# Tail of a GAT, GCN and LSTM kernel: which pairs are summed in PSUM, and where additions and stores stand

## The reference

```
h = jnp.maximum(_layernorm(x), 0.0)
x = x + _L0_gnn_ref(h, adj, W, a)             # graph attention
h = jnp.maximum(_layernorm(x), 0.0)
x = x + _L1_gnn_ref(h, adj, ...)
# _L1_gnn_ref: two graph convolutions give h, then
for p in range(1, 5):                         # windows of p nodes
    last = _lstm_last(Wih[p-1], Whh[p-1], bih[p-1], bhh[p-1], windows(h, p))
    h = h.at[:, idx, :].set(last)             # the last node of each window
```

## Time and profile before

| | |
|---|---|
| median of 3 runs | 450.65 us (450.28 to 450.68) |
| the profiled execution, own time | 451.49 us |
| its span | 449.5 us |
| outside the span | 1.99 us |
| PE busy | 426.2 us (95%) |
| DVE busy | 376.1 us (84%) |
| ACT busy | 333.6 us (74%) |
| last round, its first product on PE | 395.03 us |
| last gate product on PE | 436.63 us |

### The profile page before, as it was taken

One profiled execution on the slowest core, in us unless ns is written; L12 is line 12 of the kernel. 1 busy time (PEld: TensorE's weight loads), 2 busy tenths in 40 slices (PEclk: granted clock), 3 DMA queues, 4 the chain that ended last, 5 costly groups with the idle time before them and its releaser, 6 DMA issues.

```text
span 449.5 us, 7890 instructions
## 1 busy us (share of the span) xinstructions
PE 426.2 (95%) x2472; PEld 369.0 (82%) x2472; DVE 376.1 (84%) x994; ACT 333.6 (74%) x651; POOL 67.3 (15%) x145
## 2 busy tenths in 40 slices
PE   5689999979999999999999999999999999999995
PEld 4468788878888888888778888899999988887884
DVE  5999999987778787877778888878888789888995
ACT  3779999966899999897787768667767675574552
POOL 3678442240411313100000000000000000000000
PEclk9989999989999999999999999999999999999999
DMA  8910000000000000000000000000000000002116
GB/s 244 335 56 1 1 3 0 0 1 0 2 0 2 0 0 0 0 0 0 1 1 1 0 1 1 0 2 0 1 1 1 2 0 0 1 23 71 47 47 188
DMA packets 14212, 11.67 MB, mean 26 GB/s; under 512 B 1123, under 2 KB 12390, under 8 KB 13926
## 3 DMA queue, kind: packets, MB, share of 16 engines
q1 hardware_dynamic: 12118, 10.11, 7.5%
q10 hardware_dynamic: 2064, 1.18, 1.0%
HBM read 7.10 MB, written 4.19 MB: 25 GB/s over the span
## 4 chain that ended last, share of the span: by engine, by line
PE 69%; DVE 21%; ACT 4%; issue 3%; DMA 1%; DVEq 1%; POOL 0%; ACTq 0%; POOLq 0%
PE ps L1044 45%; PE ps L1188 12%; PE ps L1192 6%; DVE score L760 5%; DVE score L726 4%; DVE xs L774 3%; DVE stats L675 2%; PE ps L1090 2%; DVE stats L716 2%; ACT v_norm L510 1%; PE ps L1024 1%; ACT work L635 1%; PE ps L1135 1%; DMA xs<-in_x 1%; PE ps L1114 1%
## 5 line engine op out<-in xcount | busy, mean ns | idle before, releaser
L635 ACT ACTIVATE work<-ps,bl 128x512 f32<-128x512 f32 (+2 forms) x204 | 111.1, 628 | 26.9 <-PE ps L1192 19.3
L1044 PE MATMUL ps<-h_hi,wl_hi 128*128 128x512 f32 (+3 forms) x252 | 93.5, 371 | 0.9 <-DVE xs L916 0.8
L1044 PE MATMUL ps<-h_hi,wl_lo 128*128 128x512 f32 (+3 forms) x252 | 92.8, 368 | 0.0
L1044 PE MATMUL ps<-h_lo,wl_hi 128*128 128x512 f32 (+3 forms) x252 | 92.7, 368 | 0.0
L625 ACT ACTIVATE work<-work 128x512 f32<-128x512 f32 (+2 forms) x56 | 31.5, 571 | 45.1 <-DVE work L911 34.6
L510 ACT ACTIVATE v_norm<-xs,shift,scale 128x128 f32 (+1 forms) x128 | 52.7, 490 | 2.6 <-POOL shift L425 2.6
L1044 PEld LDWEIGHTS ps<-h_hi,wl_hi 128*128 128x128 f32 x252 | 47.5, 188 | 8.3 <-issue 1.2
L1044 PEld LDWEIGHTS ps<-h_lo,wl_hi 128*128 128x128 f32 x252 | 47.4, 188 | 6.6
L1044 PEld LDWEIGHTS ps<-h_hi,wl_lo 128*128 128x128 f32 x252 | 47.5, 188 | 5.6
L1188 PE MATMUL ps<-s_hi,wl_hi 128*128 128x512 f32 (+2 forms) x144 | 51.7, 362 | 0.0
L1188 PE MATMUL ps<-s_hi,wl_lo 128*128 128x512 f32 (+2 forms) x144 | 51.2, 358 | 0.0
(11 more groups left out here) (136 smaller groups left out, 911.7 us busy)
## 6 DMA issues: line engine op xcount, KB each, us to landing
result<-xs SPq DMA_DIRECT2D x12, 256.0 KB, 2.3
work<-in_w_ih_t SPq DMA_DIRECT2D x1, 1024.0 KB, 10.4
work<-in_w_hh_t SPq DMA_DIRECT2D x1, 1024.0 KB, 9.4
xs<-in_x SPq DMA_DIRECT2D x2, 256.0 KB, 3.8
xs<-in_x SPq DMA_DIRECT2D x1, 512.0 KB, 7.2
result<-xs SPq DMA_DIRECT2D x4, 128.0 KB, 2.5
result<-xs ACTq DMA_DIRECT2D x4, 128.0 KB, 2.8
adj_raw<-in_adj ACTq DMA_DIRECT2D x1, 256.0 KB, 6.8
```

Source lines behind the costliest of these rows:

```text
L635: nc.scalar.activation(lw[:, par, g, 0:cols], ps[:, 4 * par + g, 0:cols], ACT.Tanh if g == G else ACT.Sigmoid, bias=bl[:, (p - 1) * GATES ...
L1044: ins = nc.tensor.matmul(dst, a, b, start=start and n_ == 0, stop=stop and n_ == 2)
```

## The change

Five things are edited, all in the last round and behind it.

- `SUMMED` is [9, 11] in the place of [8, 9, 15]; 8 and 15 are transposed and added by VectorE, 11 is summed in PSUM. `HALVED` is [12, 13] in the place of [12, 13, 15, 14].
- PE: in the last round nothing is turned at step (0, 0); the transposes of pair 0 stand ahead of those of pair 1 in step (0, 1). Behind the round the order of the pairs is new.
- VectorE: `add_pair(0)` moves from step (0, 0) to behind the cell of step (0, 1). Of the last step's two joins, the one of half 1 moves ahead by a half step, beside that of half 0; in its old place, beside the last tanh, stands `add_pair(8)`. Behind `result_h(END, 1)` follow the additions of 10 and 12 to 15.
- ScalarE copies 9, stores the upper halves of 12 and 13, copies 11 and stores 15.
- SP stores 8, 10, 9, the lower halves of 12 and 13, 14 and 11.

```diff
-        SUMMED = [8, 9, 15]
-        HALVED = [12, 13, 15, 14]
+        SUMMED = [9, 11]
+        ADDS = [q for q in range(PAIRS) if q not in SUMMED]
+        HALVED = [12, 13]
         def added(q):
             if q in SUMMED:
                 return e_out, SUMMED.index(q) + 1
-            return d_out, q + 1 - sum(e < q for e in SUMMED)
+            return d_out, ADDS.index(q) + 1
...
-            for q in range(PAIRS - len(HALVED)):
+            for q in list(range(WITHIN)) + [8, 10, 9]:
                 store(q, 0, 4)
             for q in HALVED:
                 store(q, 0, 2)
+            store(14, 0, 4)
+            store(11, 0, 4)
...
-            for n_, q in enumerate(SUMMED):
-                act.wait_ge(e_sum, n_ + 1)
-                nc.scalar.activation(xs[:, q * 4:q * 4 + 4, :].rearrange("p k f -> p (k f)"), ps[:, bank_out(q), :],
-                                     ACT.Copy).then_inc(e_out, 1)
-            for q in HALVED:
-                act.wait_ge(*added(q))
-                act.dma_start(out_v[:, q * 4 + 2:q * 4 + 4, :], xs[:, q * 4 + 2:q * 4 + 4, :]).then_inc(stored, 16)
+            copy_out(9)
+            for q in HALVED:
+                store(q, 2, 4)
+            copy_out(11)
+            store(15, 0, 4)
...
                 full_h(r, 0, 0)
-                if r == END:
-                    add_pair(0)
...
                         cell(r, k, par)
-                        if p == LAST and k > 0:
+                        if p == LAST and k > 0 and (r, k, par) != (END, LAST - 1, 1):
                             join(r, k - 1, par)
+                        if (r, k, par) == (END, LAST - 1, 0):
+                            join(r, k - 1, 1)
                         if r == END and (k, par) == (0, 1):
+                            add_pair(0)
                             add_pair(1)
...
+            add_pair(8)
             result_h(END, 1)
-            for q in range(WITHIN, PAIRS):
-                if q not in SUMMED:
-                    add_pair(q)
+            for q in (10, 12, 13, 14, 15):
+                add_pair(q)
...
-                        if r == END:
+                        if r == END and (k, par) != (0, 0):
                             q = 2 * k + par
-                            if q in (0, 4):
+                            if q in (1, 4):
                                 pe.wait_ge(c_h[q // 4], h_base[r])
                             if k > 0:
                                 pe.wait_ge(c_act[1 - par], acts_before(r, k - 1 + par) + 1)
+                            if q == 1:
+                                transpose_pair(0)
                             transpose_pair(q)
...
             pe.wait_ge(c_act[0], a_total - 1)
-            residual(8)
             pe.wait_ge(c_h[0], h_total)
-            sum_pair(8)
+            transpose_pair(8)
+            transpose_pair(10)
             residual(9)
             sum_pair(9)
-            transpose_pair(10)
             pe.wait_ge(d_out, WITHIN)
-            transpose_pair(11)
+            residual(11)
             pe.wait_ge(c_act[1], a_total - 1)
-            residual(15)
             pe.wait_ge(c_h[1], h_total)
-            transpose_pair(12)
-            sum_pair(15)
-            transpose_pair(13)
-            transpose_pair(14)
+            for q in range(12, PAIRS):
+                transpose_pair(q)
+            sum_pair(11)
```

More of the change, by code:

```diff
@@ L658, in _, with copy_out, store @@
             cell_tanh(len(ROUNDS) - 1, LAST - 1, 1)
-            for n_, q in enumerate(SUMMED):
-                act.wait_ge(e_sum, n_ + 1)
+            def copy_out(q):
+                act.wait_ge(e_sum, SUMMED.index(q) + 1)
                 nc.scalar.activation(xs[:, q * 4:q * 4 + 4, :].rearrange("p k f -> p (k f)"), ps[:, bank_out(q), :],
                                      ACT.Copy).then_inc(e_out, 1)
+            def store(q, lo, hi):
+                act.wait_ge(*added(q))
+                act.dma_start(out_v[:, q * 4 + lo:q * 4 + hi, :], xs[:, q * 4 + lo:q * 4 + hi, :]).then_inc(stored, 16)
+            copy_out(9)
             for q in HALVED:
-                act.wait_ge(*added(q))
-                act.dma_start(out_v[:, q * 4 + 2:q * 4 + 4, :], xs[:, q * 4 + 2:q * 4 + 4, :]).then_inc(stored, 16)
+                store(q, 2, 4)
+            copy_out(11)
+            store(15, 0, 4)
         @block.vector
```

## The result

The changed kernel takes 454.18 us (median of 8 runs, 452.0 to 455.15) against 450.61 us for the kernel before (median of 8, 448.84 to 451.64): a ratio of 1.008, with a 95% interval of 1.0059 to 1.0102. It is slower by 3.6 us, and its time lies 0.2 us above the upper end of the forecast range. The direction was right and both pauses that the forecast worked out are there; the size was not, since two costs of over 1 us each came on top, one inside the span in every trace taken, one outside it in a part of the runs.

A forecast was written before the change was run, and what follows sets the result against it. The prediction took the last round on PE, then the queue of stores on full DMA engines, as the bound. Entry 1.20 plus tail 0.35 gave 1.55 us, moving the median from 450.65 to 452.2 us; range 451.0 to 454.0.

The forecast's parts named there:

- both pauses that the forecast worked out: PE idle about 2.1 us ahead of gate F of step (1, 0); DMA engines empty 0.76 us after the first store.
- The pause at gate F: Entry of the last round, step (1, 0): PE waits 2.11 us for VectorE's later addition of pair 0.
- What comes back at (1, 1): PE's old wait for the addition of pair 2 disappears, so step (1, 1) slips 1.20 us, not 2.11.
- The fallen clock: Rival, 13%: behind PE's pause the clock drops to 1.2 GHz for 3.2 us, costing 1.6 us; time 453.8 us.
- The tail: Stores behind the last round: transfers end at 448.92 us against 448.58, 0.35 us later.
- The first store 0.15 us sooner: Behind the last round: pair 8's store goes out at 439.86 us, before at 440.01.
- The hole of 0.76 us: DMA engines empty between pairs 8 and 10, as pair 10's addition stands behind `result_h`; 0.27 us was lost before.
- The work taken off PE being worth nothing: Tail: 1.3 us less PE work gains nothing by itself, since PE's end lies under the stores in both kernels.
- whole stores save 0.3 us: Last stores: by the page, four halves at 341 in place of 285 GB/s save 0.3 us; rows did not bear it out.
- the sum: Whole kernel: 1.20 + 0.35 = 1.55 us on the profiled span, 449.5 to about 451.05; median to 452.2 us.
- The rivals at 10% and 6%: 10%: no store hole, tail worth -0.5 us, time 451.35; 6%: entry costs nothing, only the tail's 0.35 left, 451.0.
- the one at 6%: Rival "Faster", 6%: PE not held at gate F, up to 0.91 us of the (1, 1) wait goes; 449.2 or 450.1 us.

The follow-up runs named there:

- filled: The changed kernel with nine extra 512-column products (gate O of step (1, 0)) on PE in place of its pause: 451.76 us, ratio 1.0058.
- stores_only: The kernel before with only the change's kinds of stores (12 and 13 in halves, 14 and 15 whole), computation as before: 450.24 us, ratio 0.9999.

## Why the prediction was wrong

**The pause at gate F** (forecast 2.11 us, released by the addition of pair 0): right, 2.08 us. **What comes back at (1, 1)** (0.91 us): right; filled, which has the wait without the fall of the clock, is 1.15 us later at the last gate product, against 1.20.

**The fallen clock** is the step that failed. It was a rival with 13% and a price of 1.6 us, and it is what happened, in all three traces with the bare pause: a granted clock of about 0.5 over some 3.3 us, 1.5 to 1.6 us lost. What was used against it was that PE had run transposes ahead of the one pause of that length in the trace of before, and wide gate products ahead of this one. That distinction had no row behind it, and there is not one such pause in the trace but two: the other, 2.06 us ahead of 9.32 us, has no fall behind it. One fall in two was about the right chance; the pause of the earlier trace rows itself turned out to bring it in 11 of 20 traces. A chance of one half in the place of 13% would have set 452.2 and 453.8 side by side. The prediction left the term at nothing, and it measured 1.5 to 1.6 us.

**The tail** (forecast +0.35 us): right, 0.37 us in both traces of the change. The first store 0.15 us sooner: 0.14 (3.24 us behind the last gate product, before 3.38 us). The hole of 0.76 us: 0.75. The work taken off PE being worth nothing: as far as the full DMA engines behind the hole show, right. The same tail with the entry of before came to 0.87 us (0.54 in the order 8, 9, 10), with slow issues on SP's queue, so the exact agreement is in part luck. The estimate that the prediction works out from the Trainium skill, page "DMA: Bandwidth & Descriptors", section "Bandwidth", that whole stores save 0.3 us, is not borne out: stores_only has its end of span where before has it (12.88 and 12.87 us behind the last gate product).

**Outside the span** (nothing forecast) is the second step that failed: the sum was made on the profiled execution's span and took the 2 us around it as fixed. They are fixed for the kernel before, and are not for this tail: 10 of 14 runs of the change have 1.1 to 1.8 us more. It is this term that carried the time over the range: the median of the eight spans, 450.95 us, with 2.0 us outside as before would be 453.0 us, inside it. Together, 1.20 + 1.56 + 0.37 = 3.1 us in the span and on average 1.0 us outside (1.4 us in 10 of 14 runs) make 4.1 us; the means differ by 3.5 us in the first eight runs and by 4.0 us in the six later ones. What sets off the part outside is not settled.

**The chances.** The rivals at 10% and 6% are counted as 0.17, and the one at 6% as 0.05; the sums are 0.16 and 0.06. Nothing hangs on it.

## What to carry to other kernels

When an edit delays the release of a shared bank, look at who waits on it in order, and price the wait together with what the engine's clock does behind it: here 0.6 us more of pause, from 1.43 to 2.08, cost 2.17 us between two traces. Look up every pause of that length in the trace, not the first one found, and in more than one trace: the same pause brought the fall in some executions and not in others. When stores are bound by the DMA engines, look at the first store, at the order on the issuing queue against the order in which the data become ready, and at how long the issues take; work taken off a compute engine was worth nothing here. Compare the whole time with the span in several runs, since a part of a loss can lie where no trace looks.

## What the runs showed of the hardware

- PE's granted clock at the entry of the last round, after idle stretches between products of 512 columns: 1.00 after 0.76 us and after 1.43 us (one trace for the latter), 0.50 for some 3.3 us after 2.08 to 2.10 us (three traces of three), from 0.3 to 1.3 us behind the end of the pause on. With nine extra products in the same stretch it stayed at 1.00 (one trace).
- The same pause does not always bring the fall: behind 2.06 to 2.07 us at the end of the attention stage the clock fell to 0.50 in 11 of 20 traces and stayed at 1.00 in 9. What decides it is not shown.
- The issue of a 256 KB store by SP took 0.37 us on an idle queue, and up to 1.97 us behind others; one such issue let the DMA engines run dry.
- The time outside the span was 1.97 to 2.07 us in 155 of 155 runs of the kernel before, and 2.8 to 3.8 us in 52 of 110 runs of nine kernels with the new tail. It was 1.98 to 2.28 us in 24 of 24 runs with more work on PE or VectorE under the last transfers, on a chip on which the version without that work was not run.
